# One sample's block in a three-engine software pipeline: VectorE adds both halves of the middle tile's pairs, the first norm's sums and scale are made a step ahead, and the third score goes to the logits' bank

## The chip, the cores and the metric

The kernel runs on one core of a Trainium2 chip. The metric is the device time in microseconds of one execution, as the median of several runs. Engines are named as the profile names them: PE is TensorE (matmul), PEld its weight load, DVE VectorE, ACT ScalarE, POOL GpSimd, SP the queue of SyncE that issues most DMAs.

## The reference

There are 16 samples of 374 tokens (in three tiles of 128, 128 and 118) with 256 channels. Each sample goes through three stages, all in float32:

```python
h = gelu(x_tokens @ W_other + x_first @ W_read + b)          # token stage
z = layernorm(h)                                             # first norm
sim = (z @ z.T) / max(|z_i| |z_j|, 1e-8)
h = h + softmax(sim) @ z + z                                 # cosine attention
y = layernorm(h)                                             # second norm
logits = (y/|y|) @ (S/|S|) - sigmoid(gates)                  # 8 experts
m = (logits > 0), or the top two where none is               # mask
r = softmax over the masked experts
q, k, v = sum_e m[t,e] * (y @ {q,k,v}_proj[e])               # 128 wide
o = causal_softmax(q @ k.T / sqrt(128)) @ v
h = h + sum_e (m*r)[t,e] * (o @ o_proj[e])                   # output
```

## The kernel before

Every product is computed in float16 with operands split in a high and a low part (three matmuls for one product), so each tensor that feeds PE has a "high" copy (mostly ACT) and a "low" remainder (DVE or POOL). The block runs as a software pipeline over steps `i`: in one step, sample `g1 = i+1` gets its first norm and its cosine products, sample `f = i` finishes cosine attention, its second norm and its routing, sample `m = i-1` gets its 24 projection units `M(0..23)` (8 experts for q, then v, then k), and sample `n = i-2` gets scores, softmax, values and the output. Each engine has its own hand-written order for a step, and semaphores tie them together. `pipeline` runs steps 1 and 2 written out, a hardware loop for steps 3 to 14, and then steps 15, 16 and 17 written out.

The order of PE in a step is `M(0)`, `dots(f,2)`, `M(1)`, `score(n,0)`, `score(n,1)`, `M(2)`, `turn_exp(f)`, `score(n,2)`, `M(3)`, `attend` x3, `M(4..7)`, `probs_v(n)`, `M(8,9)`, then twelve `pair(n,p)` between the other units, with `logits(f)` after `M(13)`, `turn_mask(f)` after `M(17)` and `dots(g1,0)`, `dots(g1,1)` at the end. `score(n,0)` waits until DVE has added pair 11 of the sample before; `turn_exp` waits for the cosine softmax's low parts (`exp_low`, L1433); `M(7)` waits for the product of token mask and tokens of expert 7 (`mask_tokens`, L1412); `pair(n,0)` waits for the heads' low part `aoT` (L1306); `probs_v` waits for the turned probabilities `pT`.

`pT` comes in this way. DVE's `mask_scores` (L1497), then ACT's exponentials (L973, L975) make the probabilities of three tiles; POOL's `low_probs` (L789) makes their low parts, one instruction for each tile; SP's `probs_around` (L536) then turns the high part and the low part by one transposing DMA each. The second one waits for the last instruction of `low_probs`.

The token mask goes the way `logits` (PE), `route` (DVE, twenty small instructions L1369 to L1399), `turn_mask` (PE, L1917), ACT (L952), a DMA to DRAM (L467) and two broadcast DMAs back (L472), and then eight `mask_tokens` on DVE (`e = 0..3` in the step itself, `e = 4..7` in the next one).

A pair `p` is two experts of output tile `p // 4`: a 128x512 product. DVE's `add_pair` (L1317) multiplies its first 256 columns by the token's weight and adds them to `h`; ACT's `scale_pairs` (L1032) multiplies the other 256 and writes them to `prod`; POOL's `sum_products`, `sum_halves` and `add_sum` (L750, L757, L764) add a tile's four such products and then add the sum to `h`. POOL does this for the tiles 0, 1 and 2, after `route_weights`.

For the first norm DVE makes the sums (`norm_stats(0, g1)`, L1278 and L1287), between `residual(f)` and the second norm's application; POOL makes the scales from them (`norm_rows`, L660 to L674), `row_scales` and the low part (`low_1`, L711). In a step POOL's order is `low_probs(n)`, `values_low(n)` (L777), `norm_rows(1, f)`, `norm_rows(0, g1)`, `row_scales(g1)`, `low_1(g1)`, `route_weights(f)`, and the three tiles.

Of the kernel before, what the change touches and what calls it, by code (L numbers as in the profile page):

```python
# [6 lines left out]
P = 128  # L7
ALU = mybir.AluOpType
# [18 lines left out]
def audio_tower_kernel(nc, x, tok_w, tok_b, sim_matrix, gates, q_proj, k_proj, v_proj, o_proj, out):  # L27
# [19 lines left out]
    with ExitStack() as ctx:  # L47
# [325 lines left out]
        def prod_buf(n, t):  # L373

            return (t + 1) % 2 if final(n) else t % 2
# [3 lines left out]
        LAST_TRIP = B - 3  # L379

# [27 lines left out]
        def _(sp):  # L408
# [140 lines left out]
            def store(n, t):  # L549
                sp.wait_ge(s_tile_ready, n * NT + t + 1).then_inc(s_passed, 1)  # L550
# [59 lines left out]
        def _(pool):  # L610
# [44 lines left out]
            def norm_rows(n, b, scale, floor):  # L655

                sm, v, chain = small[n], moments[n][:, :, 1], (s_pool1, s_pool2)[n]
                per = 5
                pool.wait_ge((s_moments1, s_moments2)[n], NT * (b + 1)).then_inc(s_passed, 1)
                g.tensor_scalar(sm[:, 0, :], v, LN_EPS, None, ALU.add).then_inc(chain, 1)  # L660
                pool.wait_ge(chain, per * b + 1).then_inc(s_passed, 1)
                g.tensor_tensor(sm[:, 1, :], sm[:, 0, :], m_half[:, :], ALU.pow).then_inc(chain, 1)  # L662
                pool.wait_ge(chain, per * b + 2).then_inc(s_passed, 1)
                g.tensor_scalar(sm[:, 4, :], sm[:, 1, :], LN_SCALE, None, ALU.mult).then_inc((s_scale1, s_scale2)[n], 1)  # L664
                g.tensor_tensor(sm[:, 2, :], v, sm[:, 1, :], ALU.mult).then_inc(chain, 1)
                pool.wait_ge(chain, per * b + 3).then_inc(s_passed, 1)

                g.tensor_tensor(sm[:, 3, :], sm[:, 2, :], sm[:, 1, :], ALU.mult).then_inc(chain, 1)
                pool.wait_ge(chain, per * b + 4).then_inc(s_passed, 1)
                g.tensor_scalar(sm[:, 2, :], sm[:, 3, :], C * scale, floor * scale, ALU.mult, ALU.max).then_inc(chain, 1)  # L670
                pool.wait_ge(chain, per * b + 5).then_inc(s_passed, 1)
# [74 lines left out]
            def sum_products(n, t):  # L746

                pool.wait_ge(s_pair_scaled, PAIRS * n + (t + 1) * (E // 2)).then_inc(s_passed, 1)
# [4 lines left out]
            def sum_halves(n, t):  # L753

                per = 2 * NT
                pool.wait_ge(s_tile_summed, per * n + 2 * t + 1).then_inc(s_passed, 1)
                g.tensor_tensor(prod_sum[:, 2, :], prod_sum[:, 0, :], prod_sum[:, 1, :], ALU.add).then_inc(s_tile_summed, 1)  # L757

            def add_sum(n, t):

                per = 2 * NT
                pool.wait_ge(s_tile_summed, per * n + 2 * t + 2).then_inc(s_passed, 1)
                pool.wait_ge(s_pair_added, PAIRS * n + (t + 1) * (E // 2)).then_inc(s_passed, 1)
# [28 lines left out]
            def step(i, g1, f, m, n):  # L792
# [4 lines left out]
                if f is not None and not early(m):  # L797
                    norm_rows(1, f, LN_SCALE ** 4, NORM_EPS * NORM_EPS)
                if g1 is not None:
                    norm_rows(0, g1, 1.0, 1e-38)  # L800
                    row_scales(g1)
                    low_1(g1)
                if f is not None:
                    route_weights(f)
                if final(n):
                    pool.wait_ge(s_tile_summed, 2 * NT * n).then_inc(s_passed, 1)
                    sum_products(n, 0)
                    add_sum(n - 1, NT - 1)
                    pool.wait_ge(s_tile_ready, NT * n).then_inc(s_passed, 1)
# [5 lines left out]
                if n is not None and not final(n):  # L815
                    add_tile(n, 1)
# [5 lines left out]
                    else:  # L822
                        add_tile(n, 2)

# [15 lines left out]
        def _(act):  # L840
# [48 lines left out]
            def high_2(b):  # L889
# [5 lines left out]
                a.activation(xhl[1][:, 0, :, :, :], xs[1][:, :, :, :], ACT.Copy).then_inc(s_hi2, 1)  # L895
# [122 lines left out]
            def step(i, g1, f, m, n):  # L1018
                def scale_pairs(lo, hi, n=n):

                    for p in range(lo, hi) if n is not None else ():
                        t, q = p // (E // 2), p % (E // 2)
# [3 lines left out]
                        if q == 0 and t == 2:  # L1026
                            act.wait_ge(s_tile_summed, 2 * NT * n + 1)
# [1186 lines left out]
```

## Time and profile before

| what | value |
|---|---|
| median of 3 runs | 727.38 us (727.03 to 729.79) |
| the profiled execution: its time, its span | 725.99 us, 724.3 us |
| granted TensorE clock | 0.999 |
| busy: PE, DVE, POOL, ACT | 684.4, 564.4, 412.1, 347.9 us |
| one step of the loop | 41.3 us |

The profile is of one execution. PE is busy 94% of the span; matmuls are pipelined, so their shown durations overlap. A row of a timeline is: start in us, duration in us, engine, line, operation, output and inputs, how many instructions are merged, and in brackets the idle time ahead of it with what ended it. The starts are more useful than the durations, since two instructions in a row on DVE overlap by some 0.08 us in the records.

### The profile page before, as it was taken

The page shows a single profiled execution, that of the slowest core. Times are in us where ns is not written, and L with a number is a line of the kernel's source. Part 1 is how long each engine was busy: PE and PEld are TensorE (multiplying, and loading weights), DVE is VectorE, ACT ScalarE, POOL GpSimd, SP SyncE. Part 2 cuts the span into 40 slices and gives each one's busy share as a digit, 9 for nine tenths or more (in the row PEclk, how much of TensorE's full clock was granted, in tenths as well). Part 3 has the DMA queues.
Part 4 walks back from the last instruction along what each step waited for, and adds up shares of the span by engine and source line. Part 5 has one row for each costly group of instructions (what it writes and reads, how often), then busy time and mean ns, then how long its engine had stood idle before and what let it go on. Part 6 is the DMA issues. An engine that isn't in the chain of part 4 may idle for free.

```text
span 724.3 us, 17445 instructions
## 1 busy us (share of the span) xinstructions
PE 684.4 (94%) x4856; PEld 435.2 (60%) x4856; DVE 564.4 (78%) x1428; ACT 347.9 (48%) x768; POOL 412.1 (57%) x669
## 2 busy tenths in 40 slices
PE   9999999999898999999899999989899999989998
PEld 8888665565555555555656555555555555555555
DVE  5788788777969788796978877796978879685736
ACT  5877463633535363434446354343536344443444
POOL 7542425665656566566557566565656656562634
PEclk9999999999999999999999999999999999999999
DMA  9571243334242332423233242424223242331211
GB/s 245 143 184 45 77 94 60 92 53 96 50 108 58 55 86 47 113 52 91 56 70 84 46 101 54 97 48 108 58 55 86 47 113 49 92 59 39 49 66 36
DMA packets 128310, 57.29 MB, mean 79 GB/s; under 512 B 100264, under 2 KB 124056, under 8 KB 128152
## 3 DMA queue, kind: packets, MB, share of 16 engines
q1 hardware_dynamic: 127888, 56.60, 33.8%
q8 instruction: 15, 0.25, 0.2%
q10 hardware_dynamic: 392, 0.32, 0.1%
q14 instruction: 15, 0.12, 0.1%
HBM read 30.45 MB, written 9.01 MB: 54 GB/s over the span
## 4 chain that ended last, share of the span: by engine, by line
PE 55%; DVE 22%; issue 13%; POOL 5%; DVEq 1%; DMA 1%; ACT 1%; POOLq 0%; SPq 0%; ACTq 0%
PE bank L1827 46%; DVE xm L1412 8%; POOL small L662 2%; DVE region_b L1295 2%; DVE stats L1278 2%; DVE region_a L1423 2%; PE bank L1747 2%; DVE exp_hl L1433 1%; DVE h L1317 1%; PE bank L1880 1%; PE bank L1897 1%; PE bank L1893 1%; PE bank L1736 1%; PE bank L1895 1%; DVE kT L1306 1%
## 5 line engine op out<-in xcount | busy, mean ns | idle before, releaser
L1827 PE MATMUL bank<-xm,w_qkv 128*128 128x374 f16 x2304 | 410.8, 322 | 2.6 <-DVE xm L1412 2.4
L1827 PEld LDWEIGHTS bank<-xm,w_qkv 128*128 128x128 f16 x2304 | 220.9, 98 | 148.9 <-DVE xm L1412 7.4
L1412 DVE TENSOR_TENSOR xm<-xT,mask_all 128x1496 f16<-128x1496 f16 x128 | 145.8, 1144 | 7.9 <-DMA mask_all<-d_mask 7.9
L1827 PE MATMUL bank<-w_o,aoT 128*128 128x512 f16 x540 | 143.3, 379 | 7.2 <-DVE aoT L1306 7.2
L1032 ACT ACTIVATE region_c<-bank,out_w 128x256 f32<-128x256 f32 x180 | 83.3, 470 | 129.0 <-PE bank L1827 127.8
L1317 DVE SCALAR_TENSOR_TENSOR h<-bank,out_w,h 128x256 f32 (+1 forms) x180 | 86.4, 480 | 70.0 <-ACT region_c L1032 68.4
L750 POOL TENSOR_TENSOR region_c<-region_c 128x512 f32<-128x512 f32 x46 | 71.9, 1563 | 51.9 <-ACT region_c L1032 47.0
L1827 PEld LDWEIGHTS bank<-w_o,aoT 128*128 128x128 f16 x540 | 51.8, 98 | 54.9 <-issue 11.8
L789 POOL TENSOR_TENSOR exp_hl<-exp,exp_hl 128x128 f16<-128x128 f32 (+2 forms) x48 | 42.3, 882 | 28.5 <-ACT exp_hl L975 28.1
L757 POOL TENSOR_TENSOR region_c<-region_c 128x256 f32<-128x256 f32 x46 | 47.1, 1025 | 8.1 <-POOL region_c L750 7.9
L901 ACT ACTIVATE aoT<-bank 128x374 f16<-128x374 f32 x15 | 7.2, 482 | 90.4 <-PE bank L1827 90.4
L764 POOL TENSOR_TENSOR h<-region_c,h 128x256 f32 (+1 forms) x45 | 37.4, 830 | 15.2 <-POOL region_c L757 10.6
L1295 DVE TENSOR_SCALAR region_b<-h,moments,small 128x256 f32 (+1 forms) x96 | 33.8, 409 | 13.0 <-POOL small L664 13.0
L660 POOL TENSOR_SCALAR small<-moments 128x3 f32<-128x3 f32 x32 | 9.1, 285 | 59.1 <-DVE moments L1287 59.0
L1893 PE MATMUL bank<-xh_sum,exp_hl 128*128 128x257 f16 x144 | 39.5, 274 | 0.0
L1897 PE MATMUL bank<-xh_sum,exp_hl 128*128 128x257 f16 x144 | 39.3, 273 | 0.0
L1895 PE MATMUL bank<-xhl,exp_hl 128*128 128x256 f16 x144 | 39.1, 271 | 0.0
L1747 PE MATMUL bank<-w_tok,xinT 128*128 128x256 f16 x288 | 37.6, 273 | 0.7 <-ACT h L864 0.7
L925 ACT ACTIVATE region_a<-region_a,log_p,small 128x374 f32<-128x374 f32 (+2 forms) x48 | 28.4, 592 | 20.1 <-DVE region_a L1423 17.6
L1827 PE MATMUL bank<-xT 128*128 128x374 f16 (+2 forms) x288 | 37.7, 269 | 0.4 <-DVE region_a L1423 0.3
L662 POOL TENSOR_TENSOR small<-small,m_half 128x3 f32<-128x3 f32 x32 | 32.8, 1026 | 5.9 <-POOL small L660 5.9
L1278 DVE BATCH_NORM_STATS2 stats<-h 128x6 f32 (+1 forms) x96 | 35.8, 414 | 0.0
(211 smaller groups left out, 1044.0 us busy)
## 6 DMA issues: line engine op xcount, KB each, us to landing
mask_all<-d_mask SPq DMA_DIRECT2D x32, 384.0 KB, 4.2
h<-in_x_dram SPq DMA_DIRECT2D x16, 256.0 KB, 4.9
out_dram<-h SPq DMA_DIRECT2D x31, 128.0 KB
rnorm_row<-d_rnorm SPq DMA_DIRECT2D x16, 192.0 KB, 3.9
d_v<-xinT SPq DMA_DIRECT2D x14, 192.0 KB, 4.4
xinT<-d_v SPq DMA_DIRECT2D x56, 48.0 KB, 2.3
h<-in_x_dram SPq DMA_DIRECT2D x15, 112.0 KB, 5.5
out_dram<-h SPq DMA_DIRECT2D x15, 112.0 KB
```

The costliest lines, as they stand in the source:

```text
L662: g.tensor_tensor(sm[:, 1, :], sm[:, 0, :], m_half[:, :], ALU.pow).then_inc(chain, 1)
L750: g.tensor_tensor(prod_sum[:, 0:2, :], prod[:, buf, 0:2, :], prod[:, buf, 2:4, :], ALU.add).then_inc(s_tile_summed, 1)
L757: g.tensor_tensor(prod_sum[:, 2, :], prod_sum[:, 0, :], prod_sum[:, 1, :], ALU.add).then_inc(s_tile_summed, 1)
L1032: a.activation(prod[:, prod_buf(n, t), q, :], pair_bank(n, p)[:, C:2 * C], ACT.Copy, scale=weights_out(n)[:, t, 2 * q + 1:2 * q + 2]).then ...
L1278: v.bn_stats(stats[n][:, t, :], h[:, b, t, :]).then_inc((s_stats1, s_stats2)[n], 1)
L1295: v.tensor_scalar(xs[n][:, :, t, :], h[:, b, t, :].rearrange("p (c q) -> p c q", c=NC), moments[n][:, t, 0:1], small[n][:, 4, t:t + 1], AL ...
L1317: v.scalar_tensor_tensor(h[:, n, t, :], pair_bank(n, p)[:, 0:C], weights_out(n)[:, t, e0:e0 + 1], h[:, n, t, :], ALU.mult, ALU.add).then_i ...
L1412: v.tensor_tensor(xm[:, e, :, 0:T], xT[1][:, :, :, 0:T].rearrange("p a c t -> p (a c) t"), mask_all[:, e, 0:T].unsqueeze(1).broadcast_to([ ...
L1747: t_.matmul(projected(t), xinT[:, b % 2, xp, c, t * P:(t + 1) * P], w_tok[:, wp, c, :], start=(c == 0 and xp == 0 and wp == 0), stop=False ...
L1827: last = t_.matmul(dst, left[lp], right[rp], start=(starts and k == 0), stop=(stops and k == 2), skip_group_check=True)
L1893: t_.matmul(banks[t][:, 0:C + 1], high, xh_sum[:, j, 0:C + 1], start=(j == 0), stop=False, skip_group_check=True)
L1897: last = t_.matmul(banks[t][:, 0:C + 1], low, xh_sum[:, j, 0:C + 1], start=False, stop=(j == NT - 1), skip_group_check=True)
```

## The change

- **Middle tile.** For the pairs 4 to 7 ACT's scaling and POOL's tile 1 sums are gone; DVE adds both halves of the pair, each with an instruction L1317, the second behind the first. `prod` has one buffer for tile 0 and one for tile 2, so ACT waits only for the sums of the sample before.
- **First norm.** DVE makes `norm_stats(0, i+2)` after pair 7's additions (no longer in front of the second norm's application), and POOL makes `norm_rows(0, i+2)` at the end of its step, after tile 2, and so ahead of the next step's `low_probs`. Step 1 makes these for two samples. SP's `norms_out` and `norms_in` move ahead accordingly. Step 14 is now written out.
- **Order around it.** `mask_tokens(m, 7)` moves on DVE to after the second norm's sums; on PE `probs_v(n)` goes ahead of `M(7)`. The second norm's scale is no longer multiplied by a constant on POOL (one small instruction less in the chain); ACT and DVE take the constant in when they split.
- **Third score** is written to `turn[0]`, the bank of the logits, so it waits for no score to be read.

```diff
-            with loop_engine.Fori(3, B - 1) as i:
+            with loop_engine.Fori(3, B - 2) as i:
                 step(i, i + 1, i, i - 1, i - 2)
+            step(B - 2, B - 1, B - 2, B - 3, B - 4)
...
+        def whole(p):
+            return E // 2 <= p < E
+        def stats_next(i):
+            return None if isinstance(i, int) and i + 2 >= B else i + 2
@@ SP, step
+                if g is not None and not early(m):
+                    norms_out(g)
...
                 if f is not None and not early(m):
                     second_rows_around(f)
-                if g is not None:
+                if early(m):
                     norms_out(g)
-                    if early(m):
-                        first_rows_around(g)
+                    first_rows_around(g)
                     norms_in(g)
-                    if not early(m):
-                        first_rows_around(g)
+                elif g is not None:
+                    norms_in(g)
+                    first_rows_around(g)
@@ POOL, norm_rows: the second norm's scale is small[1][:, 1, :]
-                g.tensor_scalar(sm[:, 4, :], sm[:, 1, :], LN_SCALE, None, ALU.mult).then_inc((s_scale1, s_scale2)[n], 1)
+                    g.tensor_tensor(sm[:, 1, :], sm[:, 0, :], m_half[:, :], ALU.pow).then_inc(s_scale2, 1)
@@ POOL, step
+                if early(m):
+                    norm_rows(0, g1, 1.0, 1e-38)
                 if g1 is not None:
-                    norm_rows(0, g1, 1.0, 1e-38)
                     row_scales(g1)
                     low_1(g1)
                 if f is not None:
                     route_weights(f)
+                if early(m):
+                    norm_rows(0, stats_next(i), 1.0, 1e-38)
...
                 if n is not None and not final(n):
-                    add_tile(n, 1)
...
                         add_tile(n, 2)
+                        if f is not None and stats_next(i) is not None:
+                            norm_rows(0, stats_next(i), 1.0, 1e-38)
@@ ACT, scale_pairs
+                        if whole(p):
+                            continue
@@ DVE, add_pair
-                dve.wait_ge(s_pair_scaled, PAIRS * n + p + 1)
+                if whole(p):
+                    dve.wait_ge(s_pair_done, PAIRS * n + p + 1)
+                else:
+                    dve.wait_ge(s_pair_scaled, scaled(n, p))
...
+                if whole(p):
+                    dve.wait_ge(s_pair_added, added(n, p - 1) + 1)
+                    v.scalar_tensor_tensor(h[:, n, t, :], pair_bank(n, p)[:, C:2 * C], weights_out(n)[:, t, e0 + 1:e0 + 2],
+                                           h[:, n, t, :], ALU.mult, ALU.add).then_inc(s_pair_added, 1)
@@ DVE, residual and step
-                    if m is not None and k == 2:
-                        mask_tokens(m, E - 1)
...
+                    dve.wait_ge(s_limit1, g1 + 1)
+                    norm_stats(0, stats_next(i))
                     cosines(g1, 0)
...
                     residual(f, m=m)
-                    if g1 is not None:
-                        norm_stats(0, g1)
+                    mask_tokens(m, E - 1)
                     norm_apply(1, f)
...
                     pairs(6, 8)
+                    if stats_next(i) is not None:
+                        dve.wait_ge(s_limit1, g1 + 1)
+                        norm_stats(0, stats_next(i))
                     for e in range(E - 5):
@@ PE, score, pair and step
-                if i == 2:
+                if i == 2 and banks[2] is banks[0]:
                     pe.wait_ge(s_scores_out, NT * n + 1)
...
-                    score(n, 2)
+                    score(n, 2, out_bank + [turn[0]])
...
-                    M(4, 5, 6, 7)
+                    M(4, 5, 6)
                     probs_v(n)
+                    M(7)
```

## Rows read from the trace of the kernel before

**Rows 1.** The page: busy time of the engines.

```profile
PE 684.4 (94%) x4856; PEld 435.2 (60%) x4856; DVE 564.4 (78%) x1428; ACT 347.9 (48%) x768; POOL 412.1 (57%) x669
```

**Rows 2.** Timeline of PE, one step of the loop.

```profile
307.08 0.67 PE L1827 MATMUL bank<-kT,qT 128*128 128x128 f16 x6 [0.83 <-DVE h L1317]
...
309.46 0.51 PE L1880 MATMUL bank<-ident,exp_hl 128*128 128x128 f16 x6 [0.77 <-DVE exp_hl L1433]
...
314.22 3.01 PE L1827 MATMUL bank<-xm,w_qkv 128*128 128x374 f16 x18
...
318.41 1.11 PE L1827 MATMUL bank<-pT,v_tok 128*128 128x374 f16 x9
...
322.02 1.46 PE L1827 MATMUL bank<-w_o,aoT 128*128 128x512 f16 x6 [0.60 <-DVE aoT L1306]
...
333.89 0.34 PE L1917 MATMUL bank<-ident,mask 128*128 128x128 f16 x3
```

**Rows 3.** Timeline of DVE: mask products, a middle pair, the first sums.

```profile
299.47 0.97 DVE L1412 TENSOR_TENSOR xm<-xT,mask_all 128x1496 f16<-128x1496 f16 x1 [0.59 <-DMA mask_all<-d_mask]
...
300.76 1.60 DVE L1412 TENSOR_TENSOR xm<-xT,mask_all 128x1496 f16<-128x1496 f16 x1
...
307.24 1.31 DVE L1412 TENSOR_TENSOR xm<-xT,mask_all 128x1496 f16<-128x1496 f16 x1
...
311.28 0.93 DVE L1412 TENSOR_TENSOR xm<-xT,mask_all 128x1496 f16<-128x1496 f16 x1
...
313.14 1.67 DVE L1412 TENSOR_TENSOR xm<-xT,mask_all 128x1496 f16<-128x1496 f16 x1
...
318.32 1.08 DVE L1278 BATCH_NORM_STATS2 stats<-h 128x6 f32 x3
...
327.91 1.07 DVE L1317 SCALAR_TENSOR_TENSOR h<-bank,out_w,h 128x256 f32 x2 [2.00 <-ACT region_c L1032]
...
340.81 0.99 DVE L1412 TENSOR_TENSOR xm<-xT,mask_all 128x1496 f16<-128x1496 f16 x1 [0.57 <-DMA mask_all<-d_mask]
```

**Rows 4.** Timeline of POOL: tile 2, low_probs, second norm's first row.

```profile
306.27 1.48 POOL L750 TENSOR_TENSOR region_c<-region_c 128x512 f32<-128x512 f32 x1 [1.94 <-ACT region_c L1032]
307.93 1.20 POOL L757 TENSOR_TENSOR region_c<-region_c 128x256 f32<-128x256 f32 x1 [0.18 <-POOL region_c L750]
309.49 0.73 POOL L764 TENSOR_TENSOR h<-region_c,h 128x256 f32 x1 [0.36 <-POOL region_c L757]
310.24 0.43 POOL L789 TENSOR_TENSOR exp_hl<-exp,exp_hl 128x128 f16<-128x128 f32 x1
...
313.11 0.91 POOL L789 TENSOR_TENSOR exp_hl<-exp,exp_hl 128x384 f16<-128x384 f32 x1 [0.37 <-ACT exp_hl L975]
```

**Rows 5.** POOL's `norm_rows(0, g1)`: its first row, and the first after it.

```profile
322.64 0.25 POOL L660 TENSOR_SCALAR small<-moments 128x3 f32<-128x3 f32 x1
...
327.27 0.25 POOL L681 TENSOR_SCALAR small<-small 128x3 f32<-128x3 f32 x1
```

**Rows 6.** Timeline of SP: the two turning DMAs of that step.

```profile
313.18 2.64 SPq L536 DMA_TRANSPOSE pT<-exp_hl  x2
```

**Rows 7.** The view of line L536: from issue to landing, over the run.

```profile
DMA to landing us min/median/max: 2.9/3.0/4.6
```

**Rows 8.** Timelines of step 15: POOL's last low part, and PE's wait for `pT`.

```profile
644.35 1.63 POOL L789 TENSOR_TENSOR exp_hl<-exp,exp_hl 128x384 f16<-128x384 f32 x1 [0.37 <-ACT exp_hl L975]
650.55 1.12 PE L1827 MATMUL bank<-pT,v_tok 128*128 128x374 f16 x9 [1.14 <-DMA pT<-exp_hl]
```

**Rows 9.** Groups of DVE from 299 to 340: count, busy and mean, idle before.

```profile
L1317 DVE SCALAR_TENSOR_TENSOR h<-bank,out_w,h 128x256 f32 x12 | 5.8, 480 | 4.4 <-ACT region_c L1032 4.3
```

**Rows 10.** The view of line L1378: duration in ns, minimum, median, maximum.

```profile
L1378 DVE TENSOR_TENSOR lg<-lg,sig x16: 182/1502/1515, 50.5 to 661.0; 128x24 f32<-128x24 f32 x16
```

**Rows 11.** Timeline of POOL: `low_1`; DVE's L1378 starts at 329.66 beside it.

```profile
329.48 1.64 POOL L711 TENSOR_TENSOR xhl<-region_b,xhl 128x768 f16<-128x768 f32 x1
```

**Rows 12.** Timeline of PE where step 1 ends.

```profile
99.18 0.48 PE L1827 MATMUL bank<-xT 128*128 128x118 f16 x6 [0.26 <-DVE region_a L1423]
```

More of the change, by code:

```diff
@@ L373, in prod_buf, with scaled, added @@
         def prod_buf(n, t):
-            return (t + 1) % 2 if final(n) else t % 2
+            return t // 2
+        def scaled(n, p):
+            return 2 * (E // 2) * n + (p + 1 if p < E // 2 else p + 1 - E // 2)
+        def added(n, p):
+            return ADDS * n + p + 1 + min(max(p + 1 - E // 2, 0), E // 2)
+        def whole(p):
+            return E // 2 <= p < E
         SLOT = (0, 2, 1)
         LAST_TRIP = B - 3
+        ADDS = PAIRS + E // 2
+        SUMS = 2 * (NT - 1)
+        def stats_next(i):
+            return None if isinstance(i, int) and i + 2 >= B else i + 2
         def by_trip(b):
@@ L549, in store @@
             def store(n, t):
-                sp.wait_ge(s_tile_ready, n * NT + t + 1).then_inc(s_passed, 1)
+                if t == 1:
+                    sp.wait_ge(s_pair_added, added(n, E - 1)).then_inc(s_passed, 1)
+                else:
+                    sp.wait_ge(s_tile_ready, (NT - 1) * n + t // 2 + 1).then_inc(s_passed, 1)
                 rows = P if t < NT - 1 else SPLIT
@@ L753, in sum_halves @@
             def sum_halves(n, t):
-                per = 2 * NT
-                pool.wait_ge(s_tile_summed, per * n + 2 * t + 1).then_inc(s_passed, 1)
+                pool.wait_ge(s_tile_summed, SUMS * n + t + 1).then_inc(s_passed, 1)
                 g.tensor_tensor(prod_sum[:, 2, :], prod_sum[:, 0, :], prod_sum[:, 1, :], ALU.add).then_inc(s_tile_summed, 1)
             def add_sum(n, t):
-                per = 2 * NT
-                pool.wait_ge(s_tile_summed, per * n + 2 * t + 2).then_inc(s_passed, 1)
-                pool.wait_ge(s_pair_added, PAIRS * n + (t + 1) * (E // 2)).then_inc(s_passed, 1)
+                pool.wait_ge(s_tile_summed, SUMS * n + t + 2).then_inc(s_passed, 1)
+                pool.wait_ge(s_pair_added, added(n, (t + 1) * (E // 2) - 1)).then_inc(s_passed, 1)
                 g.tensor_tensor(h[:, n, t, :], prod_sum[:, 2, :], h[:, n, t, :], ALU.add).then_inc(s_tile_ready, 1)
@@ L894, in high_2 @@
                     act.wait_ge(s_turned2_hi, b)
-                a.activation(xhl[1][:, 0, :, :, :], xs[1][:, :, :, :], ACT.Copy).then_inc(s_hi2, 1)
+                a.activation(xhl[1][:, 0, :, :, :], xs[1][:, :, :, :], ACT.Copy, scale=LN_SCALE).then_inc(s_hi2, 1)
             def head_high(dst, src, done, count, ready, waits, scale):
@@ L1025, in scale_pairs @@
                             act.wait_ge(s_out_w_ready, n + 1)
-                        if q == 0 and t == 2:
-                            act.wait_ge(s_tile_summed, 2 * NT * n + 1)
-                        elif q == 0 and final(n):
-                            act.wait_ge(s_tile_summed, 2 * NT * n - (3 if t == 0 else 1))
-                        elif q == 0 and later(n):
-                            act.wait_ge(s_tile_summed, 2 * NT * n - (1 if t == 0 else 3))
+                        if q == 0 and later(n):
+                            act.wait_ge(s_tile_summed, SUMS * (n - 1) + t + 1)
                         a.activation(prod[:, prod_buf(n, t), q, :], pair_bank(n, p)[:, C:2 * C], ACT.Copy,
@@ L1077, in step @@
                         weighted_high(2)
-                        act.wait_ge(s_tile_ready, NT * n + 1)
+                        act.wait_ge(s_tile_ready, (NT - 1) * n + 1)
                         act.dma_start(out[n, 0:P, :], h[:, n, 0, :]).then_inc(s_stored, 16)
@@ L1295, in norm_apply_tile @@
                 v.tensor_scalar(xs[n][:, :, t, :], h[:, b, t, :].rearrange("p (c q) -> p c q", c=NC),
-                                moments[n][:, t, 0:1], small[n][:, 4, t:t + 1],
+                                moments[n][:, t, 0:1], small[n][:, (4, 1)[n], t:t + 1],
                                 ALU.subtract, ALU.mult).then_inc((s_xs1, s_xs2)[n], 1)
@@ L1342, in add_first_tile @@
             def add_first_tile(n):
-                dve.wait_ge(s_tile_summed, 2 * NT * n + 2)
-                dve.wait_ge(s_pair_added, PAIRS * n + E // 2)
+                dve.wait_ge(s_tile_summed, SUMS * n + 2)
+                dve.wait_ge(s_pair_added, added(n, E // 2 - 1))
                 v.tensor_tensor(h[:, n, 0, :], prod_sum[:, 2, :], h[:, n, 0, :], ALU.add).then_inc(s_tile_ready, 1)
@@ L1918, in turn_mask, with score @@
                 last.then_inc(s_mask_turned, 1)
-            def score(n, i):
+            def score(n, i, banks=out_bank + out_bank[:1]):
                 if i == 0:
@@ L1924, in score @@
                     if later(n):
-                        pe.wait_ge(s_pair_added, PAIRS * n)
-                if i == 2:
+                        pe.wait_ge(s_pair_added, ADDS * n)
+                if i == 2 and banks[2] is banks[0]:
                     pe.wait_ge(s_scores_out, NT * n + 1)
-                split_product(out_bank[i % 2][:, 0:KEYS[i]], [qT[:, p, i * P:(i + 1) * P] for p in range(2)],
+                split_product(banks[i][:, 0:KEYS[i]], [qT[:, p, i * P:(i + 1) * P] for p in range(2)],
                               [kT[:, p, 0:KEYS[i]] for p in range(2)], True, True, s_scores_done)
@@ L1992, in pair @@
                 if final(n) and p in (2, 3):
-                    pe.wait_ge(s_pair_added, PAIRS * n + p - 3)
+                    pe.wait_ge(s_pair_added, ADDS * n + p - 3)
                 if p >= ahead:
-                    pe.wait_ge(s_pair_added, PAIRS * n + p - ahead + 1)
+                    pe.wait_ge(s_pair_added, added(n, p - ahead))
                 split_product(pair_bank(n, p)[:, :], [heads_out(n)[:, k, t * P:(t + 1) * P] for k in range(2)],
```

39 lines of the change are left out of this document (24 added, 15 removed).

## The prediction

> **What bounds the kernel.** The page comes first: PE is busy 94% of the span, DVE 78%, POOL 57% [rows 1]. So a gain must come out of PE's gaps, and a loss is a new gap. Then PE's timeline. A step repeats every 340.81 - 299.47 = 41.34 us [rows 3], and PE stands still at four places in it, each time behind DVE: 0.83 us before the first score, 0.77 before `turn_exp`, 0.22 before `M(7)`, 0.60 before `pair(n,0)` [rows 2]. By starts the gaps are a little longer, since the shown ends are modelled. The step is a ring with two links. From PE's `turn_mask` the mask goes through ACT, DRAM and back, and DVE starts its first product 340.81 - 333.89 = 6.92 us later, after 0.57 us of waiting for that DMA [rows 2, 3]. From there DVE has no gap until the tokens of `M(7)`. The other link is `probs_v` (318.41) to `pair(n,0)` (322.02) to `turn_mask` (333.89): 3.61 + 11.87 us [rows 2]. I count all times of a step below from DVE's first product, t = 0 at 299.47. `probs_v` starts at t = 18.94, and 18.94 + 3.61 + 11.87 + 6.92 = 41.34 is 41.34 again, so these links close the ring.
>
> **What DVE gains and pays.** The eight halves of the middle tile are four more L1317; two of them in a row take 1.07 us [rows 3], so four cost 2.2 us. The first norm's sums, 1.08 us plus three short L1287 (some 0.3), move to the same stretch, between `turn_mask` and the first product, so it gets 3.6 us more work. DVE now waits 4.4 us in a step ahead of its twelve L1317 [rows 9], 2.00 of it ahead of `route` [rows 3], so 2.4 us in this stretch, and 0.57 for the DMA: 3.0 us. One more thing is freed: L1378 takes 182 ns at best and 1502 in the median [rows 10], and it stands beside POOL's `low_1`, 1.64 us long [rows 11]. With the scales made a step ahead, `low_1` comes some 3 us earlier in the step, and `route` gets 1.3 us shorter. So the extra work is hidden, and if `low_1` does not move it comes out a few tenths late. I take 0.
>
> **What POOL gains.** Tile 1's sums are gone. They ran beside the mask products: the second took 1.60 us where one alone takes 0.93 [rows 3]. A product runs alone in 0.93, and L757 beside one takes 1.20, while L764, of the same width, takes 0.73 [rows 3, 4]. I take 0.7 us off the second product and 0.1 off the neighbours: DVE's run is 0.8 us earlier. That takes most of PE's first gap (0.83). `turn_exp` is 0.1 to 0.2 us earlier beyond that at most. PE would then be ready for `probs_v`, which now goes before `M(7)`, at about t = 16.9: 314.22 is the start of `M(4)`, less 0.7, plus three units (the three merged ones fill 3.01 us with an overlap) [rows 2]. Taken by itself that would be a step of 16.9 + 3.8 + 11.8 + 6.9 = 39.4 us.
>
> **What POOL pays, the step that decides.** `norm_rows(0, i+2)` now stands between tile 2 and the next `low_probs`, and `low_probs` feeds the second turning DMA, for which `probs_v` waits. The moved code took 327.27 - 322.64 = 4.63 us [rows 5], nearly all of it latency of eight tiny instructions and the waits between them. Step by step:
> - Tile 2's last addition ends at 310.22, t = 10.75 [rows 4]. With DVE 0.8 earlier and the same blocks beside it I take 10.05.
> - `norm_rows`: 4.2 us without a block, as 4.63 holds one of about 0.4. Now it runs beside the mask products of experts 5 and 6 (311.28 and 313.14 in the old step) [rows 3]. The row shows what such a meeting costs: one product took 1.31 us beside a POOL instruction, and the POOL instruction beside it 1.20, so one of two waits for the other. A tiny POOL instruction that comes just behind the start of a product waits up to 0.8 us. Two meetings, in which the first or the second may wait: I take 5.3 us, end at t = 15.35.
> - `low_probs`: before, it ran with ACT from 310.24 to 314.02; now ACT is long done. 0.43 and 0.91 for the first and the third tile [rows 4], 0.65 between them for the second (estimate, in between by size): 2.0 us, end at t = 17.35 instead of 14.55.
> - The DMA: before, the second one was queued behind the first and could start 1.4 us after 313.18, t = 15.1 [rows 6]. Now it starts at 17.45 and lands 3.0 later [rows 7]. `probs_v` starts at t = 20.5 instead of 18.94: 1.56 us late, with PE idle for 3.5 us.
> - From there `M(7)`, `M(8)`, `M(9)` and then the pair: 3.8 instead of 3.61, since the 0.60 us wait for `aoT` is gone but `M(7)` is now in between: +0.18. The small wait in front of `turn_mask` goes with the shorter `route`: -0.08.
>
> Sum for a step: +1.56 + 0.18 - 0.08 = +1.66 us. `norm_rows` stands ahead of `low_probs` in the steps 3 to 14, so twelve times: +19.9 us. Step 1 gets a second set of sums ahead of `cosines`, for which PE already waits [rows 12]: +1.3 us. Step 15 has no such `norm_rows` ahead of it and keeps DVE's gain: -0.4 us. Against the profiled execution: 725.99 + 20.8 = 746.8 us. The median of the runs is 1.4 us above that execution; I say 747.5 us.
>
> The one row that shows this sensitivity is step 15 of the old kernel: the last `low_probs` instruction took 1.63 us instead of 0.91, ended at 645.98, and `probs_v` came at 650.55, 1.14 us after PE was ready [rows 8]. From the one's end to the other's start these are 4.6 us, where [rows 7] give 3.0 as the usual landing.
>
> **A rule beside the rows.** That a product and a POOL instruction beside it stretch each other is in the rows: 1.31 and 1.20 us against 0.93 and 0.73 [rows 3, 4]. The Trainium skill says in "SBUF — State Buffer", section "Who interferes with whom", that a VectorE instruction with two SBUF inputs and a GpSimd instruction that reads SBUF take an exclusive lock, and that the second to issue fully blocks, by order and not by shape. By it the 3-element instructions of `norm_rows` pay the full rest of a product, and the sum is the +19.9 above; if they only shared bandwidth, `norm_rows` would take its 4.2 us and the sum would be about 12 x 0.56 = +7 us. The same rule speaks for the change's other half: L1317 reads one operand from PSUM, so the added halves do not block POOL. L1378's two values fit the lock.
>
> **Bounds.** Low: nothing on POOL is ever blocked. Tile 2 then ends near t = 9.25 (10.75, less the 0.8 of DVE, less 1.20 - 0.73 for L757 and some 0.2 for L750), `norm_rows` at 13.45, `low_probs` at 15.45, landing at 18.5: -0.4 us a step. High: `low_probs` itself meets products, 1.63 for its third part as in step 15, and the landing stays 3.0: +0.8 more, or it takes 4.4 as there: +1.4 more.
>
> **Rivals.**
> - **POOL's chain goes unblocked, and the kernel is faster.** For it: tile 1's three POOL instructions are gone, and blocks are a matter of tenths. It decides at t = 15.75 for the end of `low_probs`; earlier than that, `probs_v` is no later than now. At the low bound: 12 x -0.4 = -5, +1 for the ends, 722 us; below 15.75 each tenth gives 1.2 us. Against it: two products of DVE stand in just that window. Chance 0.13.
> - **Half blocked:** between the bounds, 0 to +0.9 us a step: 727 to 737 us, middle 733. Chance 0.17.
> - **The forecast**, +1.2 to +2.2 a step: 741 to 753 us. Chance 0.56.
> - **The landing takes 4.4 us, as in step 15, or `low_probs` is blocked too:** 754 to 766 us, middle 760. For it: one of 14 steps shows it; against it: the others land in 3.0 [rows 7]. Chance 0.10.
> - **The change's DVE work is the price:** `low_1` stays beside L1378, and the mask products start 0.3 to 0.5 us late: +4 to +6 us, but only where `probs_v` is not late anyway: 732 us. Chance 0.04.
>
> Range: I leave out the faster end and the upper half of the slow landing: 727 to 759 us. What a measurement of this kernel can tell from no change is about 0.5%, 3.6 us (723.7 to 731.0). From the cases: faster 0.10 (most of the first rival), same 0.12, slower 0.78.
>
> **What would show it.** In the changed kernel's profile: a PE gap of some 3 us before the matmuls `bank<-pT,v_tok`, released by the DMA `pT<-exp_hl`, with `low_probs` (POOL, exp_hl) some 3 us later after the mask product of expert 4 than now. The waits of PE for `h` and `aoT` small or gone. No POOL rows of tile 1, L1378's line with a median near 182 ns, and ACT's scaling at 8 for 12 per sample. A loop step of about 43.0 us. The prediction is wrong if `norm_rows` takes 4.2 us or less there, if `low_probs` runs in less than 2.0, or if POOL reaches tile 2 more than half a microsecond earlier than I take; and it is wrong in the other direction if PE's gap is released by anything but that DMA.

## The result, and the profile after

The changed kernel takes **756.32 us** (755.04 to 757.57, four runs) where the kernel before, in four runs, takes 727.76 us (727.03 to 729.79). The ratio is 1.0388, with a 95% interval of 1.0357 to 1.0418: slower by 3.9%. The forecast was slower, 747.5 us, with a range of 727 to 759. The side was right, and so was the chain that makes the kernel slower; the size was 9 us short. 756 lies outside the forecast's own case (741 to 753 us) and is in the range only because the range took in half of a rival, a slow landing, that did not happen. The profiled execution took 755.35 us, with a span of 753.5 us.

First the page of the changed kernel: the span, the engines' busy time, the shares of the chain that ended last, and one of the costly groups.

```profile
span 753.5 us, 17078 instructions
...
PE 696.6 (92%) x4856; PEld 442.8 (59%) x4856; DVE 562.0 (75%) x1488; ACT 319.0 (42%) x708; POOL 348.0 (46%) x608
...
PE 47%; DMA 13%; POOL 13%; issue 12%; DVE 8%; ACT 4%; POOLq 1%; DVEq 1%; SPq 0%; ACTq 0%
...
L1868 PE MATMUL bank<-pT,v_tok 128*128 128x374 f16 (+2 forms) x144 | 18.2, 273 | 38.6 <-DMA pT<-exp_hl 38.5
```

Two things are to be seen. The 144 matmuls of `probs_v` were free of waits but for one of 1.1 us before, and now PE stands idle for 38.6 us ahead of them, behind the transposing DMA. And PE's busy time rose by 12.2 us against [rows 1], with the same 4856 matmuls: the same work ran slower. The first was forecast. The second was not, and it is what the prediction lacks.

PE's waits in the changed kernel, in total, their number, and the longest:

```profile
PE bank L1868 <- DMA pT<-exp_hl: 38.5, 14, 3.2
PE bank L1921 <- DVE exp_hl L1470: 10.5, 14, 0.8
...
PE bank L1868 <- DVE h L1350: 0.4, 2, 0.2
```

PE's first gap of [rows 2] (0.83 us behind `h`) is nearly gone, its wait for `aoT` is gone, and one wait has come in their place. The timeline of PE over the step that answers to [rows 2]:

```profile
318.79 0.51 PE L1921 MATMUL bank<-ident,exp_hl 128*128 128x128 f16 x6 [0.76 <-DVE exp_hl L1470]
...
323.55 3.01 PE L1868 MATMUL bank<-xm,w_qkv 128*128 128x374 f16 x18
...
329.74 1.16 PE L1868 MATMUL bank<-pT,v_tok 128*128 128x374 f16 x9 [3.18 <-DMA pT<-exp_hl]
330.70 4.69 PE L1868 MATMUL bank<-xm,w_qkv 128*128 128x374 f16 x18
...
335.22 1.46 PE L1868 MATMUL bank<-w_o,aoT 128*128 128x512 f16 x6
...
347.01 0.33 PE L1958 MATMUL bank<-ident,mask 128*128 128x128 f16 x3
```

The two rows of `xm,w_qkv` have the same 18 matmuls of one form. The one ahead of the gap takes 3.01 us, as in [rows 2], and the one behind it 4.69: 1.68 us more. What differs between them is the granted clock (below). DVE and POOL beside it; DVE's first product is t = 0, here 309.67:

```profile
309.67 0.94 DVE L1449 TENSOR_TENSOR xm<-xT,mask_all 128x1496 f16<-128x1496 f16 x1 [0.65 <-DMA mask_all<-d_mask]
```

```profile
315.60 1.49 POOL L780 TENSOR_TENSOR region_c<-region_c 128x512 f32<-128x512 f32 x1 [6.14 <-ACT region_c L1062]
...
318.89 0.73 POOL L792 TENSOR_TENSOR h<-region_c,h 128x256 f32 x1 [0.42 <-POOL region_c L786]
319.70 0.23 POOL L685 TENSOR_SCALAR small<-moments 128x3 f32<-128x3 f32 x1
...
321.19 0.52 POOL L689 TENSOR_SCALAR small<-small 128x3 f32<-128x3 f32 x1 [0.20 <-POOL small L687]
...
322.55 0.96 POOL L700 TENSOR_SCALAR small<-small 128x3 f32<-128x3 f32 x1 [0.19 <-POOL small L698]
...
324.71 1.93 POOL L817 TENSOR_TENSOR exp_hl<-exp,exp_hl 128x128 f16<-128x128 f32 x3
```

This is the chain of the forecast: tile 2 to 319.62, `norm_rows` from 319.70 to 324.74 (seven instructions, L685 to L704, and not the eight of the prediction), `low_probs` to 326.64. Two of the 3-element instructions, 0.25 us where nothing is beside them, took 0.52 and 0.96: products of DVE began at 320.68 and 322.48. The chain that ended last, for this step, shows the rest (start, duration, what it is):

```profile
326.74 2.89 DMA pT<-exp_hl
```

And the granted clock, in windows of 1 to 5 us through the same stretch (the window, its length, busy us and instructions of PE, PEld, DVE, ACT and POOL, then PE's granted clock as a share of 2.4 GHz, the DMA share and GB/s):

```profile
326.50:329.70 3.20, 0.06 (x1) 0.00 (x0) 1.00 (x2) 0.00 (x0) 2.83 (x4) 1.00 0.40 72
329.70:331.00 1.30, 1.26 (x10) 0.91 (x11) 0.99 (x3) 0.00 (x0) 0.78 (x3) 0.88 0.00 0
331.00:332.00 1.00, 1.00 (x5) 0.51 (x4) 0.46 (x1) 0.98 (x2) 0.83 (x1) 0.50 0.00 0
...
333.00:334.00 1.00, 1.00 (x5) 0.48 (x4) 0.78 (x1) 0.37 (x1) 0.48 (x2) 0.50 0.21 44
334.00:335.00 1.00, 1.00 (x8) 0.58 (x6) 0.00 (x0) 0.00 (x0) 0.37 (x2) 0.96 0.80 153
335.00:340.00 5.00, 5.00 (x29) 2.63 (x28) 2.29 (x6) 1.83 (x4) 0.00 (x0) 1.00 0.32 79
```

Through the idle stretch the records still grant 1.00. Only after `probs_v` has begun does it fall, to 0.50 (1.2 GHz), for 3.4 us (330.7 to 334.1) in which PE is busy all the time. At half the clock that is 1.7 us of work left undone, which is what the 18 matmuls show. The Trainium skill says in "TensorE: Matmul & The Clock Gate", section "Part 1: The HAM clock gate", that an idle engine is throttled to half its clock and that activity releases it; the order in these rows, idle first and then the lower level, agrees.

The same place over the whole run: the wait of PE, and then, on the chain, the 63 matmuls behind it, in the steps 3, 4 and 14.

```profile
154.21 1.12 PE L1868 MATMUL bank<-pT,v_tok 128*128 128x374 f16 x9 [2.59 <-DMA pT<-exp_hl]
...
196.73 1.27 PE L1868 MATMUL bank<-pT,v_tok 128*128 128x374 f16 x9 [3.18 <-DMA pT<-exp_hl]
...
639.80 1.12 PE L1868 MATMUL bank<-pT,v_tok 128*128 128x374 f16 x9 [3.01 <-DMA pT<-exp_hl]
```

```profile
154.21 10.36 PE bank L1868 x63
...
196.73 12.03 PE bank L1868 x63
...
639.80 10.36 PE bank L1868 x63
```

In steps 2, 3, 14 and 15 these 63 matmuls take 10.36 us, in the ten steps 4 to 13 they take 12.03: 10 x 1.67 = 16.7 us, more than half of the 28.6 us lost. The gap of step 14 is only 0.17 us shorter than that of step 4, and the clock did not fall behind it. From `turn_mask` to `turn_mask` (the last row of the timeline above) those ten steps take 44.2 to 44.4 us; the kernel before takes some 41.4.

### The profile page after: what moved, and what is told of

It reads as the page before. It is cut to its first block, busy times and chain, and to the rows that moved or that the text cites. A ratio compares the mean times of both kernels' runs of the same rounds, so it can differ in the third digit from the quotient of the medians.

```text
span 753.5 us, 17078 instructions
## 1 busy us (share of the span) xinstructions
PE 696.6 (92%) x4856; PEld 442.8 (59%) x4856; DVE 562.0 (75%) x1488; ACT 319.0 (42%) x708; POOL 348.0 (46%) x608
## 4 chain that ended last, share of the span: by engine, by line
PE 47%; DMA 13%; POOL 13%; issue 12%; DVE 8%; ACT 4%; POOLq 1%; DVEq 1%; SPq 0%; ACTq 0%
PE bank L1868 39%; DMA mask_all<-d_mask 6%; DMA pT<-exp_hl 5%; DVE xm L1449 4%; PE bank L1788 3%; POOL region_c L780 3%; POOL exp_hl L817 2%; POOL region_c L786 2%; DMA d_mask<-maskT 2%; POOL small L687 2%; POOL small L700 1%; DVE region_a L1460 1%; PE bank L1777 1%; ACT exp_hl L959 1%; DVE h L1350 1%
## 5 line engine op out<-in xcount | busy, mean ns | idle before, releaser
L1868 PE MATMUL bank<-xm,w_qkv 128*128 128x374 f16 x2304 | 425.4, 331 | 0.0
L1868 PEld LDWEIGHTS bank<-xm,w_qkv 128*128 128x128 f16 x2304 | 227.5, 100 | 154.4 <-issue 17.1
L1449 DVE TENSOR_TENSOR xm<-xT,mask_all 128x1496 f16<-128x1496 f16 x128 | 130.2, 1022 | 6.8 <-DMA mask_all<-d_mask 6.8
L1062 ACT ACTIVATE region_c<-bank,out_w 128x256 f32<-128x256 f32 x120 | 54.9, 468 | 128.9 <-PE bank L1868 128.0
L780 POOL TENSOR_TENSOR region_c<-region_c 128x512 f32<-128x512 f32 x31 | 43.3, 1395 | 105.6 <-ACT region_c L1062 100.8
L741 POOL TENSOR_TENSOR xhl<-region_b,xhl 128x768 f16<-128x768 f32 x16 | 26.3, 1644 | 70.7 <-ACT xhl L917 70.7
L1868 PE MATMUL bank<-pT,v_tok 128*128 128x374 f16 (+2 forms) x144 | 18.2, 273 | 38.6 <-DMA pT<-exp_hl 38.5
L984 ACT ACTIVATE maskT<-bank 8x384 f16<-8x384 f16 x16 | 7.6, 477 | 85.7 <-PE bank L1958 85.7
L1868 PEld LDWEIGHTS bank<-pT,v_tok 128*128 128x128 f16 x144 | 12.2, 98 | 47.7 <-issue 38.5
L817 POOL TENSOR_TENSOR exp_hl<-exp,exp_hl 128x128 f16<-128x128 f32 (+2 forms) x48 | 34.0, 730 | 10.8 <-ACT exp_hl L1007 10.8
```

Source lines behind the costliest of these rows:

```text
L780: g.tensor_tensor(prod_sum[:, 0:2, :], prod[:, buf, 0:2, :], prod[:, buf, 2:4, :], ALU.add).then_inc(s_tile_summed, 1)
L817: done = g.tensor_tensor(probs_tile(1, i), full, probs_tile(0, i), ALU.subtract)
L1062: a.activation(prod[:, prod_buf(n, t), q, :], pair_bank(n, p)[:, C:2 * C], ACT.Copy, scale=weights_out(n)[:, t, 2 * q + 1:2 * q + 2]).then ...
L1449: v.tensor_tensor(xm[:, e, :, 0:T], xT[1][:, :, :, 0:T].rearrange("p a c t -> p (a c) t"), mask_all[:, e, 0:T].unsqueeze(1).broadcast_to([ ...
L1868: last = t_.matmul(dst, left[lp], right[rp], start=(starts and k == 0), stop=(stops and k == 2), skip_group_check=True)
```

## The experiments

Each ran beside the kernel before on its chip: 728.59 us for the first four, 731.13 us for the others.

**1. The scale back in its old place.** The sums stay a step ahead on DVE and the middle tile stays on DVE; only `norm_rows(0, ...)` and its rows' DMAs return to the step that uses them.

```
-                if early(m):
-                    norm_rows(0, g1, 1.0, 1e-38)
                 if g1 is not None:
+                    norm_rows(0, g1, 1.0, 1e-38)
                     row_scales(g1)
...
-                        if f is not None and stats_next(i) is not None:
-                            norm_rows(0, stats_next(i), 1.0, 1e-38)
```

> The changed kernel, with norm_rows(0, g1) back at its old place on POOL, between norm_rows(1, f) and row_scales(g1), and norms_out back ahead of norms_in on SP. The sums are still made a step ahead by DVE. Theory (POOL's chain ahead of low_probs is what costs): the low probabilities are again paced by ACT, the second turning DMA lands near t = 17.3, PE's wait for pT falls from 3.2 us to under 0.6, no stretch of the step runs at a lower granted clock, a step takes 40 to 40.5 us, and the kernel 707 to 715 us, under the kernel before. Rival (DVE's added work or the middle tile is the cost): PE's gap moves to a wait for DVE and the time stays at 728 us or more.

Measured: 713.39 us (711.86 to 714.35), ratio 0.9779 (0.9747 to 0.9812). A step takes 40.45 us and the clock stays whole, as expected. PE's waits:

```profile
PE bank L1915 <- DVE exp_hl L1464: 10.5, 14, 0.8
PE bank L1862 <- DMA pT<-exp_hl: 9.6, 14, 1.3
PE bank L1862 <- DVE h L1344: 3.6, 12, 0.6
```

Seven small instructions at another place of POOL's queue are worth 43 us against the changed kernel, and without their move the rest of the change is a gain of 2.2%. The wait for `pT` is 0.7 us a step instead of 3.2, a little more than the 0.6 expected.

**2. The gap filled.** The changed kernel, with 14 matmuls of 384 columns put between `M(6)` and `probs_v` that write a score bank whose contents have been used up. They make nothing earlier; they only keep PE at work in the gap.

```
                     M(4, 5, 6)
+                    pe.wait_ge(s_scores_out, NT * n + 1)
+                    for k in range(14):
+                        t_.matmul(out_bank[0][:, 0:TP], qT[:, 0, 0:P], kT[:, 0, 0:TP], ...)
                     probs_v(n)
                     M(7)
```

> The changed kernel, with 14 extra matmuls of 384 columns (2.3 us of work, their output is never read) between M(6) and probs_v. They add nothing that anyone waits for; pT still lands at the same time. Theory (in ten of the steps the idle time of 3.2 us lets the granted clock fall, and the next 3.4 us of matmuls run at 1.2 GHz): the clock stays at 1.00, each of ten steps loses 1.67 us, 739 to 742 us. Rival (the stretch after probs_v is slow for another reason, as transposing DMAs beside it): 755 to 758 us.

Measured: 742.42 us (741.41 to 742.78), ratio 1.0183 (1.0150 to 1.0216). The landing is as late as in the changed kernel (`probs_v` again at t = 20.1), and what is left of the gap is short:

```profile
326.62 1.12 PE L1868 MATMUL bank<-pT,v_tok 128*128 128x374 f16 x9 [0.92 <-DMA pT<-exp_hl]
```

The step falls from 44.3 to 42.6 us, by the 1.7 us of the clock, and the granted clock is 1.0 over the whole run. So useless work makes the kernel 14 us faster. It would be some 17, but in the steps 2 and 15, where the changed kernel's gap is 0.5 us, the fill itself costs 1.6 us each (44.6 and 41.4 us instead of 43.0 and 39.8). This splits the loss: the lateness itself costs +1.2 us a step over the 41.4 of before, the clock +1.7.

**3. The middle tile alone.** The kernel before, with only the middle tile's pairs on DVE (sums, scale, order and the third score's bank as they were).

```
         def prod_buf(n, t):
-            return (t + 1) % 2 if final(n) else t % 2
+            return t // 2
...
-                    add_tile(n, 1)
```

with `scale_pairs`, `add_pair`, `sum_products` and `store` as in the changed kernel.

> The kernel before, with the middle tile's eight halves on DVE alone and nothing else of the change. Theory: DVE's run of mask products is 0.7 to 0.8 us earlier since POOL's tile 1 is gone, the 2.2 us of added work lie in DVE's idle time, PE's wait for h before the first score nearly goes: 12 x 0.7 = 8 us less, 717 to 721 us. Rival (the added halves hold up route or the mask products): 727 us or more.

Measured: 709.76 us (708.93 to 710.66), ratio 0.9741 (0.9710 to 0.9772): 18.8 us gained, where I had expected 8 (717 to 721 us). Most steps take 39.8 to 40.0 us, the others 40.45. Two neighbouring steps show which of the two it is; DVE's first product and POOL's last addition for tile 0 beside it, in the first step and in the second:

```profile
293.96 0.94 DVE L1432 TENSOR_TENSOR xm<-xT,mask_all 128x1496 f16<-128x1496 f16 x1 [0.47 <-DMA mask_all<-d_mask]
...
334.04 1.46 DVE L1432 TENSOR_TENSOR xm<-xT,mask_all 128x1496 f16<-128x1496 f16 x1 [0.73 <-DMA mask_all<-d_mask]
```

```profile
294.15 1.33 POOL L780 TENSOR_TENSOR h<-region_c,h 128x256 f32 x1 [0.43 <-POOL region_c L774]
...
333.97 0.73 POOL L780 TENSOR_TENSOR h<-region_c,h 128x256 f32 x1 [0.43 <-POOL region_c L774]
```

Where the product starts 0.19 us ahead, POOL's addition takes 1.33 instead of 0.73; where the addition is 0.07 us ahead, the product takes 1.46 instead of 0.94. The Trainium skill, "SBUF — State Buffer", section "Who interferes with whom", says that the second to issue waits, whatever the shapes; this pair agrees. What the expectation left out is further down the step: tile 2 on POOL is earlier, so `low_probs`' third part falls in behind the product of expert 6 (306.96 against 306.92), and that product takes 0.93 us, not the 1.67 of [rows 3].

**4. The unit ahead of `probs_v` again.** The changed kernel with its old order on PE, which puts 1 us of work into the gap.

```
-                    M(4, 5, 6)
+                    M(4, 5, 6, 7)
                     probs_v(n)
-                    M(7)
```

> The changed kernel with PE's old order M(4, 5, 6, 7), probs_v. pT lands as before, so 0.95 us of PE's idle time is filled by a unit that was due behind it: the gap is 2.2 us instead of 3.2. If the length of the gap is what lets the clock fall, both come back, 12 x 0.95 + 10 x 1.67 = 28 us, 728 to 731 us. If the clock falls all the same after 2.2 us: 743 to 746 us. If M(7) then waits for DVE's later product of expert 7, up to 5 us more in either case.

Measured: 733.31 us (731.79 to 735.62), ratio 1.0067 (1.0042 to 1.0091). It lies between the two values expected, because the clock fell in only four of the eleven steps 4 to 14. The gap is now two short ones, and the first of them is `M(7)`'s wait for the product of expert 7, which the change has put later in DVE's order. The first two rows are a step in which the clock fell behind them, the third is the second gap of the next step, in which it did not:

```profile
318.61 1.12 PE L1868 MATMUL bank<-xm,w_qkv 128*128 128x374 f16 x6 [0.93 <-DVE xm L1449]
...
320.88 1.94 PE L1868 MATMUL bank<-pT,v_tok 128*128 128x374 f16 x9 [1.14 <-DMA pT<-exp_hl]
...
364.39 1.12 PE L1868 MATMUL bank<-pT,v_tok 128*128 128x374 f16 x9 [1.12 <-DMA pT<-exp_hl]
```

```profile
321.80:322.80 1.00, 1.00 (x8) 0.81 (x7) 0.01 (x1) 0.00 (x0) 0.77 (x2) 0.50 0.00 0
...
365.30:366.30 1.00, 1.00 (x11) 0.64 (x8) 0.21 (x2) 0.67 (x2) 0.73 (x2) 1.00 0.00 0
```

A step with the fall takes 43.2 to 43.5 us, one without it 41.6 to 41.9: 1.7 us again. So for this landing the order `M(7)`, then `probs_v` is 23 us better than the order that the change brings. The old order keeps PE at work while the DMA flies.

**5. The norm a step ahead alone.** The changed kernel with the middle tile as before, on POOL.

```
         def prod_buf(n, t):
-            return t // 2
+            return (t + 1) % 2 if final(n) else t % 2
...
                 if n is not None and not final(n):
+                    add_tile(n, 1)
```

with `scale_pairs`, `add_pair`, `sum_products` and `store` as in the kernel before.

> The changed kernel without its middle tile: ACT scales and POOL sums tile 1 as before; the norm a step ahead, the orders and the third score stay as changed. Theory (the moved norm_rows alone is the loss; the middle tile on DVE is a gain by itself, whichever scale order it goes with): DVE's run and POOL's tile 2 are 0.7 us later than in the changed kernel, so pT is too, PE's gap is 3.2 us or more and the clock falls in most steps: 762 to 768 us. Rival (the two parts only cost together, because DVE's added halves hold up the chain): under 745 us.

Measured: 777.92 us (773.51 to 781.22), ratio 1.0631 (1.0583 to 1.0679). This part holds the whole loss, and the direction of the expectation held. The time is 10 us above the upper end expected, some 3 of them this chip's (731.13 us for the kernel before, 727.76 in the first measurement). The waits of PE:

```profile
PE bank L1863 <- DMA pT<-exp_hl: 38.9, 14, 3.2
PE bank L1863 <- DVE h L1349: 15.6, 14, 1.3
```

The steps alternate between 45.5 and 46.65 us. From `probs_v` to `pair(n,0)` it is 5.47 us in one and 6.66 in the next: the clock stayed low for longer in every second step, which the expectation did not have. Windows of a step of the first and of the second kind:

```profile
341.00:342.00 1.00, 1.00 (x6) 0.57 (x5) 0.69 (x5) 0.42 (x2) 0.45 (x3) 0.74 0.00 0
...
382.70:383.20 0.50, 0.00 (x0) 0.00 (x0) 0.00 (x0) 0.00 (x0) 0.50 (x1) 0.50 0.29 28
...
387.40:388.40 1.00, 1.00 (x5) 0.47 (x4) 0.95 (x1) 0.48 (x1) 1.00 (x1) 0.50 0.04 8
388.40:389.40 1.00, 1.00 (x5) 0.52 (x4) 0.00 (x0) 0.00 (x0) 0.26 (x2) 0.54 0.97 189
```

In the first step `probs_v` began at 337.99, the clock fell behind it, and it was on its way back between 341 and 342. In the second `probs_v` began at 383.45, but the clock had fallen ahead of it, inside the gap (382.70), and it came back only at 389.3. PE then worked at the lower level from 383.45 to 389.3, 5.9 us, and half of that is the 2.9 us that this step's 6.66 is above the 3.80 of the full clock. The gaps themselves are alike, 3.2 us at most.

**6. The third score's bank alone.** The kernel before, with its third score in the logits' bank.

```
-                    score(n, 2)
+                    score(n, 2, out_bank + [turn[0]])
...
-                    mask_scores(n, 2, out_bank[0])
+                    mask_scores(n, 2, turn[0])
```

> The kernel before with only the third score moved to the logits' bank. Both theories: no wait of the step rests on that bank; the wait that goes was over some 0.8 us before PE came to it. No change, 726 to 730 us.

Measured: 731.46 us (730.39 to 733.42), ratio 1.0006 (0.9989 to 1.0024). No change; the kernel before takes 731.13 us on this chip, which is why the time is above the 726 to 730 expected.

**7. The middle tile with the shorter scale of the second norm.** Experiment 3 plus one more piece of the change: the second norm's constant factor goes out of `norm_rows(1, ...)`, into ACT's scale and DVE's `low_2`. The first norm stays as it was, in its own step.

```
-                per = 5
+                per = (5, 4)[n]
...
-                a.activation(xhl[1][:, 0, :, :, :], xs[1][:, :, :, :], ACT.Copy).then_inc(s_hi2, 1)
+                a.activation(xhl[1][:, 0, :, :, :], xs[1][:, :, :, :], ACT.Copy, scale=LN_SCALE).then_inc(s_hi2, 1)
```

> The kernel before with the middle tile on DVE and the second norm's scale without the constant (one small POOL instruction and its wait less in front of the second norm's application). Theory: DVE comes to aoT 0.4 us earlier, PE's wait of 0.26 us for it goes in each step: 3 us under the middle tile alone, 706 to 708 us. Rival (aoT is paced by ACT's high part there): 709 to 711 us.

Measured: **707.90 us** (706.83 to 708.85), ratio 0.9683 (0.9659 to 0.9708). This is the fastest version, 3.2% under the kernel before. PE's waits that are left:

```profile
PE bank L1908 <- DVE exp_hl L1459: 10.6, 14, 0.8
PE bank L1855 <- DVE h L1339: 4.0, 9, 0.7
PE bank L1945 <- DVE lg L1425: 3.4, 11, 0.3
```

The wait for `aoT` is 0.2 us in all (4.0 in experiment 3).

**8. Experiment 1 with the old order too.** The sums still a step ahead, the scale in its old place, `M(7)` ahead of `probs_v`, and the product of expert 7 ahead of the residual again.

```
-                    M(4, 5, 6)
+                    M(4, 5, 6, 7)
                     probs_v(n)
-                    M(7)
...
+                    if m is not None and k == 2:
+                        mask_tokens(m, E - 1)
...
                     residual(f, m=m)
-                    mask_tokens(m, E - 1)
```

> As e1 (norm_rows back in its old place, sums a step ahead, middle tile on DVE), but with the old order of M(7) and probs_v on PE and of the product of expert 7 on DVE. Theory: pT has 0.95 us more before PE asks for it, so the wait of 0.72 us that e1 shows goes, and nothing takes its place: 8 us less than e1, 704 to 707 us. Rival (PE then waits as long for the product of expert 7 or for aoT): 710 to 714 us.

Measured: 712.06 us (710.25 to 712.27), ratio 0.9730 (0.9705 to 0.9754), above the 704 to 707 expected. The wait for `pT` is gone, as expected, but others stand in its place:

```profile
PE bank L1953 <- DVE lg L1430: 6.3, 11, 0.6
PE bank L1863 <- DVE h L1344: 4.1, 10, 0.6
```

All its runs are slower than all those of experiment 7 on the same chip (710.25 to 712.27 us against 706.83 to 708.85), which has no sums a step ahead, though the intervals of the two ratios touch. So taking the sums a step ahead brings nothing here even when the scale is out of POOL's way: PE then waits for the mask (`lg`) 0.6 us a step instead of 0.3.

Together with experiments 1 and 4 this also says what the place of `norm_rows` costs in either order of PE. With `probs_v` ahead of `M(7)` it is 1.0388 against 0.9779, some 44 us; with `M(7)` first it is 1.0067 against 0.9730, some 25 us. So 43 us is not the price of the seven instructions alone, but of them and of a PE order that leaves the gap open. (Experiment 4 left the product of expert 7 in its new place on DVE, experiment 8 did not.)

## Why the prediction was right, and where it fell short

By the prediction's own steps, with t counted from DVE's first product:

- **What DVE gains and pays.** DVE's run came out as taken: the first product waits 0.65 us for its DMA, and the second one lasts 0.93 us instead of 1.60. I took its extra work at 0, and DVE is not what holds up the first product: that still waits for its DMA, for no shorter time than before (0.65 us, 0.57 in [rows 3]). `turn_mask` to the next first product is 7.06 us, forecast 6.92; where these 0.14 us come from was not looked into. L1378's counterpart has a median of 184 ns, as said:

```profile
L1415 DVE TENSOR_TENSOR lg<-lg,sig x16: 182/184/185, 49.8 to 691.0; 128x24 f32<-128x24 f32 x16
```

- **POOL reaches tile 2 earlier.** Forecast t = 10.05 for its end; measured 319.62 - 309.67 = 9.95.
- **`norm_rows` with two meetings.** Forecast 5.3 us; measured 5.04, with exactly two instructions drawn out (by 0.27 and 0.71 us). The moved code has seven instructions, where I counted eight; the sum goes by its duration and not by the count. By the rule of the exclusive lock in the Trainium skill, "SBUF — State Buffer", section "Who interferes with whom", this was to be expected, and the trace agrees.
- **`low_probs`.** Forecast 2.0 us; measured 1.93. By its letter this is one of the prediction's signs of being wrong ("less than 2.0"); at 0.07 us it is the rounding of an estimate, and the chain stands. End at t = 16.97, forecast 17.35.
- **The DMA.** Forecast 3.0 us to landing; measured 2.89. `probs_v` at t = 20.07, forecast 20.5: late as said, by 1.13 us and not 1.56.
- **From `probs_v` to `pair(n,0)`: the term that was mis-sized.** The prediction has 3.8 us, "3.8 instead of 3.61". Measured: 335.22 - 329.74 = 5.48. I had put PE "idle for 3.5 us" in the line above and gone on at the matmul times of [rows 2], which are times at the full clock. The clock fell, and the same matmuls took 1.68 us more. Experiment 2 shows the cause: with the gap filled and the DMA just as late, the 1.7 us are gone.
- **`pair(n,0)` to `turn_mask`.** Forecast 11.79 (11.87 less 0.08); measured 347.01 - 335.22 = 11.79.

The sum for this step is 20.07 + 5.48 + 11.79 + 7.06 = 44.40 us, against the 43.0 forecast: -0.43 for `probs_v`, +1.68 for the clock, +0.14 for the last link. Over the run: the fourteen steps 2 to 15, each from one `turn_mask` to the next, take 30.7 us more than before, of which 16.7 are the ten falls of the clock. The other 14.0 are the lateness, for which the forecast had 1.3 + 19.9 - 0.4 = 20.8. The lateness was some 1.25 us a step in the steps 5 to 13 and less in the steps 3 and 4 (+0.5 each) and 14 (+1.1), not 1.66 in all twelve; step 2, where `region_a` now holds PE up, cost 2.3 instead of 1.3. So I had the lateness 7 us too dear and the clock not at all, and the two errors partly cancel: that the number is only 9 us off is in part luck. (The sum by its own terms is 748.2 us, 746.8 and the 1.4 for the median; I said 747.5.) The parts outside these fourteen steps give back 1.5 us. Step 15, forecast at -0.4, gained 1.6 us (39.8 us from mask to mask): besides DVE's gain the old kernel's own wait there of 1.14 us [rows 8] is down to 0.54, which my sum did not count.

The rivals: that POOL's chain goes unblocked, or is half blocked, fell with the two drawn-out instructions and the end of `low_probs` at t = 16.97, behind the deciding 15.75. A slow landing (754 to 766 us) names a time near the measured one for the wrong reason: the longest landing of the changed kernel is 3.5 us. The view of the two turning DMAs' line:

```profile
DMA to landing us min/median/max: 2.9/2.9/3.5
```

That DVE's work is the price fell with the zero above. The part of the change that I treated as a small gain, 0.8 us of DVE, is worth more than that alone: experiment 3 gains 18.8 us.

Still open is why the second landing in step 15 of the old kernel took 4.4 us. No version here was made to ask it.

## What to carry to other kernels

Before a chain of tiny instructions is moved to a "free" place on an engine's queue, look at what is behind it there: here seven 3-element instructions ahead of the work that feeds a DMA cost more than the whole rest of the change gains. When a forecast contains an idle stretch of PE of a few microseconds, the matmuls after it cannot be priced at the times from before it; read PE's granted clock around such gaps, and put other ready work into them, since even useless matmuls paid here. Before a unit is moved behind a wait, ask whether it was what kept PE at work during it: that one swap was 23 us here. Test the parts of a change apart: this one held a gain of 2.6%, a loss of 6.3% and a part worth nothing.

## What the runs showed of the hardware that was not expected

- The clock fell late: after 3.18 us of idleness PE ran some 0.9 us at the full clock (329.74 to 330.7), and then until 334.1 at 1.2 GHz. After 2.59 us (step 3) and after 3.01 us (step 14) it did not fall, but it did with a gap of 3.00 us in step 14 of experiment 5 (`probs_v` at 659.74, 5.08 us to the pair instead of 3.81), where PE had also waited 1.27 us some 13 us earlier. So the length of the gap alone does not decide; what else does was not measured.
- A fall cost half of the time that PE worked at the lower level: 1.7 us for 3.4, and 2.9 us for 5.9 (experiment 5).
- Two gaps of 0.93 and 1.14 us with one unit of 1 us between them brought it down in four of eleven steps; gaps of the same size did not in the others. Single gaps of 0.92 us (experiment 2) never did.
- After gaps of the same size it fell at two different moments, in turns (experiment 5): behind the start of `probs_v`, and then it was back at 341.5, or inside the gap, and then the lower level lasted from 382.5 to 389.3. What decides between them stays open.
- A difference of 0.26 us in who comes first, a product of DVE or an addition of POOL, moves 0.5 us from one engine to the other, and with it a whole step by 0.6 us (experiment 3).
